# Two attention layers joined: layer 2's last batch and layer 3's first two steps in one sequence of instructions

## The reference, cut to what matters

```
x = layernorm(x + L0(x, adj))   # 8 Euler steps of a linear graph ODE
x = layernorm(x + L1(x, adj))   # graph convolution, two batch norms over all batches and nodes
x = layernorm(x + L2(x, adj))   # 4-head attention masked by adj, head size 32
x = layernorm(x + L3(x, adj))   # one-head graph attention

L3:  Wh = h @ W;  s1 = Wh @ a1;  s2 = Wh @ a2
     e = leaky_relu(s1[:, :, None] + s2[:, None, :], 0.2), masked where adj == 0
     out = softmax(e) @ Wh
```

## Time and profile before

| | |
|---|---|
| median of 3 runs | 1016.34 us (1015.45 to 1021.12) |
| profiled execution | 1015.21 us, its span 1013.3 us |
| PE, DVE, ACT, POOL busy | 90%, 64%, 49%, 38% |
| mean granted TensorE clock | 0.952 of 2.4 GHz |

### The profile page before, as it was taken

One profiled execution on the slowest core, in us unless ns is written; L12 is line 12 of the kernel. 1 busy time (PEld: TensorE's weight loads), 2 busy tenths in 40 slices (PEclk: granted clock), 3 DMA queues, 4 the chain that ended last, 5 costly groups with the idle time before them and its releaser, 6 DMA issues. The chain is left out here.

```text
span 1013.3 us, 20934 instructions
## 1 busy us (share of the span) xinstructions
PE 911.3 (90%) x6036; PEld 643.4 (63%) x6036; DVE 646.4 (64%) x2016; ACT 501.3 (49%) x900; POOL 388.1 (38%) x440
## 2 busy tenths in 40 slices
PE   6999999999999899764799999999999937999994
PEld 5799999999998788332454455444544415667663
DVE  4745554555455866464567777777777415988984
ACT  4321212212112355553477777777776624767762
POOL 4001021111111210002367777778777640455445
PEclk9999999999999999895699999999999977999997
DMA  8000000000000000000342423333333300010111
GB/s 234 21 11 12 22 12 18 13 10 21 10 0 18 22 0 1 0 0 1 68 90 65 94 63 84 72 80 77 78 79 78 80 3 1 22 31 21 31 31 31
DMA packets 34217, 40.63 MB, mean 40 GB/s; under 512 B 6656, under 2 KB 17536, under 8 KB 34176
## 3 DMA queue, kind: packets, MB, share of 16 engines
q1 hardware_dynamic: 33072, 40.00, 16.5%
q10 hardware_dynamic: 1104, 0.13, 0.1%
HBM read 6.43 MB, written 4.19 MB: 10 GB/s over the span
## 5 line engine op out<-in xcount | busy, mean ns | idle before, releaser
L1319 DVE CUSTOM_DVE_ANT_0 junk<-bank,mask_ij 128x512 bf16<-128x512 f32 x256 | 166.7, 689 | 82.7 <-PE bank L1396 81.1
L1199 POOL TENSOR_TENSOR half_sum<-prob 128x1024 f32<-128x1024 f32 x64 | 151.8, 2381 | 11.6 <-ACT prob L1262 11.6
L1262 ACT ACTIVATE prob<-wide 128x1024 f32<-128x1024 f32 x128 | 125.2, 1017 | 37.8 <-PE wide L1413 32.5
L424 ACT CAST yT<-wide 128x512 fp32r<-128x512 f32 x48 | 28.1, 588 | 206.2 <-PE wide L809 156.8
L1396 PE MATMUL bank<-qkT 32*128 32x512 f32 x256 | 66.9, 518 | 20.5 <-DVE mx L1319 17.8
L519 POOL TENSOR_TENSOR Xr<-Xf,Xr 128x512 fp32r<-128x512 f32 x16 | 20.4, 1291 | 168.1 <-ACT Xr L419 167.9
L152 POOL TENSOR_SCALAR n_rstd<-n_aggr 128x4 f32<-128x4 f32 x32 | 6.7, 209 | 198.6 <-DVE n_aggr L145 186.6
L1409 PE MATMUL wide<-qk_st 128*128 128x512 f32 x256 | 76.7, 422 | 0.7 <-ACT prob L1262 0.3
L1732 PEld LDWEIGHTS bank<-Wh,pr 128*128 128x128 f32 x512 | 61.1, 196 | 23.8 <-issue 19.9
L1732 PE MATMUL bank<-Wh,pr 128*128 128x129 f32 x512 | 65.3, 282 | 10.9 <-ACT pr L1600 10.9
L58 PE MATMUL bank<-z,L3T_hi 128*128 128x256 f32 x256 | 73.3, 286 | 1.0 <-DVE z L625 0.9
(11 more groups left out here) (282 smaller groups left out, 2278.9 us busy)
## 6 DMA issues: line engine op xcount, KB each, us to landing
qk_st<-qkT SPq DMA_DIRECT2D x192, 128.0 KB, 2.4
out_dram<-rc SPq DMA_DIRECT2D x16, 256.0 KB, 2.3
Xf<-X SPq DMA_DIRECT2D x14, 256.0 KB, 2.3
A<-in_adj_dram SPq DMA_DIRECT2D x4, 256.0 KB, 5.2
qk_st<-neg_row SPq DMA_DIRECT2D x64, 2.0 KB
Xf<-in_x_dram SPq DMA_DIRECT2D x2, 256.0 KB, 6.7
mask_q<-mask_ji SPq DMA_DIRECT2D x16, 32.0 KB, 1.8
w<-in_L_gnn_W_dram SPq DMA_DIRECT2D x2, 128.0 KB, 2.2
```

The lines of the kernel that those rows point to most:

```text
L1199: pool.tensor_tensor(flat(half_sum[h][:]), flat(prob[bp][h][:, 0:2]), flat(prob[bp][h][:, 2:4]), ALU.add).then_inc(h_sum, 1)
L1262: act.activation(flat(prob[bp][h][:, 2 * half:2 * half + 2]), wide[half][:], ACT.Exp, scale=SCALE).then_inc(t_exp, 1)
L1319: dve.tensor_tensor_reduce(out=junk[hh][:], in0=bank[4 + hh][:], in1=m.mask_ij[:, i], scale=1.0, scalar=3.0 * MASKED, op0=ALU.add, op1=ALU ...
```

## The change

Layers 2 and 3 share one block (`layers2_3`). Each engine runs layer 2's steps up to 17 or 18 as before, then a list written out by hand (`tail`), in which words with a leading 3 are items of layer 3 (`3x0.1` is item x0 of batch 1) and the others items of layer 2, and then layer 3's loop from step 2. Layer 3's large buffers lie at fixed places over layer 2's input `m.O`, over `qk_st` and over `qkT`. Layer 3's weights are loaded and prepared in layer 0's last step: two more transfers on SP behind that of `m.W2`, a wait and a transpose at the end of TensorE's `#w`, a copy on VectorE, a small matmul and copy (`#v`), and two copies on ScalarE that spread the columns. The items of layer 3 are otherwise unchanged, and its waits for layer 2 are three: all Exps of batch 15 ahead of its first transpose, the norm of the batch that GpSimd copies, and the last use of `m.O`.

```diff
--- before.py
+++ after.py
-def pairs(eng, steps, depth, step):
+def pairs(eng, steps, depth, step, first=0, last=None):
...
-    for s in range(lead):
+    for s in range(first, lead):
...
-    for s in range(steps, steps + depth - 1):
+    for s in range(steps, steps + depth - 1 if last is None else last + 1):
...
-            "PE": order("#t0 #t1 #t2 #t3 #w0 p p p p #A0 #A1 #A2 #A3 p p p p"),
+            "PE": order("#t0 #t1 #t2 #t3 #w0 p p p p #A0 #A1 #A2 #A3 p p p p #v0"),
             "ACT": order("z z z z #t0 #t1 #t2 #t3 #x0 #x1 z z z z #A0 #A1 #A2 #A3"),
-            "DVE": order("z z N z z A #m0 #m1 p p #m2 #m3 #G0 p p #D0 z z z z #A0 #x0 #x1 #w0 p #A1 p #A2 p #A3 p n #a0 a"),
+            "DVE": order("z z N z z A #m0 #m1 p p #m2 #m3 #G0 p p #D0 z z z z #A0 #x0 #x1 #w0 p #A1 p #A2 p #A3 p n #v0 #a0 a"),
         }
...
-        LATE = {"PE": ORDER, "ACT": ORDER, "DVE": order("N #x2 #a1 A")}
+        LATE = {"PE": ORDER, "ACT": order("#v0"), "DVE": order("N #x2 #a1 A")}
...
+            sp.dma_start(m.WX[:, 0:D], ins["L3_gnn_W"]).then_inc(w3_in, 16)
+            with nc.allow_non_contiguous_dma(reason="256 words once"):
+                sp.dma_start(L1.a3[:], ins["L3_gnn_a"].rearrange("(k p) a -> p (k a)", p=P)).then_inc(w3_in, 16)
...
+            sp.wait_ge(w3_in, 2 * 16)
...
+                    elif what == "#v":
+                        act.wait_ge(wa_c, 1)
+                        for n in range(2):
+                            act.activation(m.wB[n][:], m.WX[:, D + n:D + n + 1].broadcast_to([P, P]), ACT.Copy).then_inc(wb_c, 1)
...
+                        dve.wait_ge(wt_ps, 1)
+                        dve.tensor_copy(L1.W3T[:], bank[3][:, 0:D]).then_inc(wt_c, 1)
+                    elif what == "#v":
+                        dve.wait_ge(wa_ps, 1)
+                        dve.tensor_copy(m.WX[:, D:D + 2], bank[3][:, 0:2]).then_inc(wa_c, 1)
...
+                        pe.wait_ge(w3_in, 2 * 16)
+                        pe.transpose(bank[3][:, 0:D], m.WX[:, 0:D], m.ident[:]).then_inc(wt_ps, 1)
+                    elif what == "#v":
+                        pe.wait_ge(wt_c, 1)
+                        pe.matmul(bank[3][:, 0:2], L1.W3T[:], L1.a3[:], start=True, stop=True).then_inc(wa_ps, 1)
...
+        m.WX = at("WX", [P, D + 2])
+        m.wB = [at(f"wB{k}", [P, P]) for k in range(2)]
...
+def layer3(nc, own, m, bank, out, rl1_at, ready):
...
+    at = [172352]
...
+    WX, wB = m.WX, m.wB
+    Xf = [over(f"Xc{k}", [P, NT, D]) for k in range(2)]
+    xT = [over(f"xTc{k}", [P, N]) for k in range(2)]
+    Wh = [over(f"Wh{k}", [P, NT, D + 2]) for k in range(2)]
+    junk = [over(f"junk3{k}", [P, N], BF16) for k in range(2)]
+    dg = [over(f"dg{k}", [P, NT, P], BF16) for k in range(2)]
+    r = [over(f"rc{k}", [P, NT, D]) for k in range(2)]
+    onesb = over("onesb", [P, P], BF16)
+    rl = [over("rl0", [P, NT, N]), nc.alloc_sbuf_tensor_at("rl1", [P, NT, N], F32, offset=rl1_at)]
+    at[0] = 205120
+    pr = [over(f"pr{k}", [P, NT, N]) for k in range(2)]
+    s12 = [sb(f"s12{k}", [P, NT, 2]) for k in range(2)]
+    s2s = [sb(f"s2s{k}", [P, 2, NT]) for k in range(2)]
...
+    def pool_constants(pool):
+        pool.sem_inc(x_f, CREDIT)
+        norm.credit_pool(pool)
+        norm.credit_apply(pool)
+        pool.wait_ge(*ready["O"])
+        for n, ap in enumerate((onesb[:], Wh[0][:, :, D:D + 1], Wh[1][:, :, D:D + 1])):
+            pool.memset(ap, 1.0).then_inc(const, 1)
+
+    def pool_copy(pool, s, par, first=False):
+        pool.wait_ge(x_ps, after(s - 2, 1))
+        pool.wait_ge(ready["X"], after(s, 4))
+        if not first:
+            pool.wait_ge(norm.s_x, after(s - 4, 4))
+        hold(pool, gate)
+        pool.tensor_copy(flat(Xf[par][:]), batch_flat(m.X, s)).then_inc(x_f, 1)
+
+    def pool_norm(pool, b, par, copied):
+        pool.wait_ge(x_f, after(copied, 1))
+        norm.root(pool, b + CREDIT, par)
+        norm.apply(pool, b + CREDIT, par, r[par], lambda k: r[par][:, k])
+
+    def pool_rest(pool):
...
+                if isinstance(s, int) and s == 0:
+                    pe.wait_ge(*ready["score banks"])
...
+        third = layer3(nc, own, m, bank, out, qkT_at,
+                       {"O": (bn, after(B - 1, 1)), "X": norm.s_x, "score banks": (t_exp, after(B - 1, EXPS))})
...
+        def tail(text, items, second, third_item):
+
+            backs = dict(items)
+            for word in text.split():
+                name, b = word.split(".")
+                b = int(b)
+                if name[0] == "3":
+                    s = b + third.STAGE[name[1]]
+                    third_item(name[1], int(name[2]), s, s % 2, s // 2)
+                else:
+                    s = b + backs[name]
+                    second(name, b, b % 2, s, [0 <= s - k < B for k in range(6)])
 
...
-            run(pool, POOL_ORDER, work)
+            run(pool, POOL_ORDER, work, last=17)
+            third.pool_constants(pool)
+            for b in range(2):
+                third.pool_copy(pool, b, b, first=True)
+            tail("r.14 S2.15 S3.15 g2.14", POOL_ORDER, work, None)
+            third.pool_copy(pool, 2, 0, first=True)
+            tail("r.15 g2.15", POOL_ORDER, work, None)
+            third.pool_copy(pool, 3, 1, first=True)
+            third.pool_norm(pool, 0, 0, 3)
+            third.pool_rest(pool)
...
-            run(act, ACT_ORDER, work)
+            run(act, ACT_ORDER, work, last=18)
+            third.act_credits(act)
+            item = third.act_items(act)
+            tail("3x0.0 f.15 3w0.0 3w1.0 y.14 3l0.0 3l1.0 e.15 3l2.0 3l3.0 3g0.0 3x0.1 3w0.1 3w1.1 3E0.0 3E1.0 "
+                 "3l0.1 3l1.1 3l2.1 3l3.1 3g0.1 y.15", ACT_ORDER, work, item)
+            pairs(act, B, 3, third.in_order(item), first=2)
...
-            run(dve, DVE_ORDER, work)
+            run(dve, DVE_ORDER, work, last=17)
+            third.dve_credits(dve)
+            item = third.dve_items(dve)
+            tail("b.14 3w0.0 3w1.0 3m0.0 3m1.0 3m2.0 3m3.0 3c0.0 3c1.0 3c2.0 c1.15 c2.15 3e0.0 3e1.0 3w0.1 3w1.1 b.15 "
+                 "3e2.0 3e3.0 3m0.1 3m1.1 3m2.1 3m3.1 3c0.1 3c1.1 3c2.1", DVE_ORDER, work, item)
+            pairs(dve, B, 3, third.in_order(item), first=2)
...
-            run(pe, PE_ORDER, work)
...
+            run(pe, PE_ORDER, work, last=18)
+            third.pe_credits(pe)
+            item = third.pe_items(pe)
+            pe.wait_ge(third.const, 3)
+            tail("3x0.0 V0.15 V1.15 V2.15 V3.15 3w0.0 3w1.0 3j0.0 3i0.0 o.15 D0.15 D1.15 3x0.1 d.15 3w0.1 3w1.1 3e0.0 3e1.0 "
+                 "3j0.1 3i0.1 3e2.0 3e3.0", PE_ORDER, work, item)
+            pe.wait_ge(rcp, after(B - 1, 1))
+            pe.wait_ge(o_n, after(B - 1, 1))
+            pairs(pe, B, 3, third.in_order(item), first=2)
...
```

More of the change, by code:

```diff
@@ L277, in layer0 @@
         blocks_in = sem("mask_blocks_in"); const = sem("rows_set")
+        w3_in = sem("w3_in"); wt_ps = sem("WT_in_psum"); wt_c = sem("WT_out"); wa_ps = sem("Wa_in_psum"); wa_c = sem("Wa_out")
+        wb_c = sem("Wa_spread")
         Hb, Xa, agT, W1T = L1.Hb, L1.Xr, L1.agT, L1.W1T
@@ L908, in aggregate_step @@
                         pe.wait_ge(la_w_lo, 1)
+                        pe.wait_ge(wa_c, 1)
                         pe.wait_ge(h_sb, after(groups - 1, 2 * NT))
@@ L957, in __init__ @@
         self.wf = at("wf", [P, CH, P])
+        self.a3 = at("a_sb", [P, 2])
+        self.W3T = at("WT", [P, D])
         self.at = 170304
@@ L1066, in layer2, with layers2_3 @@
+def layers2_3(nc, m, bank, wide, out):
     SCALE = float(HD) ** -0.5
@@ L1079, in layer2 @@
         xTr = [sb(f"xT_{h}", [P, N], F32R) for h in ("hi", "lo")]
+        qkT_at = nc.sbuf_base
         qkT = [sb(f"qkT{k}", [P, 4, N], F32R) for k in range(2)]
@@ L1135, in released, with run @@
                     "o": (o_n, after(b, 1)), "T": (res1, after(b, 1))}[name]
-        def run(eng, items, act_on):
+        def run(eng, items, act_on, last=None):
             depth = 1 + max(back for _, back in items)
@@ L1144, in step @@
                         act_on(name, s - back, (par + back) % 2, s, alive)
-            pairs(eng, B, depth, step)
+            pairs(eng, B, depth, step, last=last)
+        def tail(text, items, second, third_item):
[6 more added lines that the diff above has]
+                    third_item(name[1], int(name[2]), s, s % 2, s // 2)
+                else:
+                    s = b + backs[name]
+                    second(name, b, b % 2, s, [0 <= s - k < B for k in range(6)])
         @block.sync
@@ L1172, in _ @@
             run(sp, SP_ORDER, transfer)
+            third.sync(sp)
         @block.gpsimd
@@ L1755, in build @@
             layer1_rest(nc, second, m, bank, L1)
-            layer2(nc, m, ins, bank, wide)
-        layer3(nc, m, ins, bank, out)
+            layers2_3(nc, m, bank, wide, out)
 _INS = ["x", "adj", "L0_gnn_alpha_train", "L0_gnn_w", "L0_gnn_d", "L0_gnn_fc_in_w", "L0_gnn_fc_in_b",
```

479 lines of the change are left out of this document (216 added, 263 removed).

## The result

| | before | after |
|---|---|---|
| median of 4 runs each, us | 1015.89 (1013.87 to 1021.12) | 1000.87 (995.78 to 1005.56) |
| profiled execution, its span, us | 1015.21, 1013.3 | 995.78, 994.0 |
| mean granted clock of TensorE in it | 0.952 | 0.967 |

The medians differ by 15.0 us. The ratio of the times, after over before, is 0.9839 with a 95% interval of 0.9803 to 0.9876, so the gain is clear of no change and between 1.2% and 2.0%. The forecast was 1002, range 995.5 to 1009.

A forecast was written before the change was run, and what follows sets the result against it. The layer 2 to 3 stretch was held bound by latency, not an engine; -21.3 + 0.3 + 3.0 + 3.3 + 0.5 = -14.2 us from 1015.2 gave 1001.0, stated as 1002 against the runs' median, range 995.5 to 1009.

The forecast's parts named there:

- join without the clock: Layer 2's last Exp to layer 3's first `a`: 20.7 us in place of 42.0, so 21.3 less.
- y.15 in step 2: Layer 3's step 2: ScalarE runs y.15 (1.65 us) ahead of batch 2's input copy; 0.3 us is left as cost.
- clock in three gaps: TensorE's clock may fall behind three idle times in the join; +3.0 us taken, bounds 0 and 4.6.
- wait for `a` in layer 0: Layer 0: TensorE waits for the last-issued transfer, so products `p` start 3.3 us late; bounds 0 and 5.6.
- other pieces in layer 0: Layer 0: an added VectorE copy and small matmul, with ScalarE's copies within the bounds; +0.5 us, bounds 0 and 1.
- orders that are passed: Join: items moved ahead of others, such as GpSimd's memsets and copies, cost 0, bounds 0 and +1 us.
- the transfer is hidden: Rival in layer 0: the weights' transfer costs nothing, the 3.3 us fall away, 998.8 us; chance 0.14.
- gap 3: TensorE idle ahead of layer 3's first `a`, 3.4 us; a clock fall there would cost 1.5 to 1.9 us.
- gap 1: TensorE idle ahead of batch 0's transposes, 2.1 us; a clock fall would cost about half of 1.4 us.
- gap 2: TensorE idle ahead of batch 1's projections, 2.4 us; a clock fall would cost about half of 1.4 us.
- cold loop: Rival: layer 3's loop from step 2 stays at low clock, +6.7 us per step, 1022 after three; chance 0.04.
- interlocked orders: Rival in the join: in-order queues wait on each other in turn, wholly or in half, 1007 to 1015; chance 0.11.

The follow-up runs named there:

- in_turn: Changed kernel, still one block, but each engine runs all of layer 2's list before layer 3's; 1013.61 us, ratio 0.9964 to the kernel before.
- two_gaps: Changed kernel with layer 3's weight transfers issued earlier and unread matmuls (9, 8) in TensorE's first two join gaps only; 994.90 us, ratio 0.9778 to before.
- all_together: Changed kernel with earlier weight transfers, three join gaps filled, y.15 and b.15 moved later, sums' masks ahead of score rows; 997.17 us, ratio 0.9781 to before.
- fill_gaps: Changed kernel plus 9, 8 and 11 unread matmuls in TensorE's three idle gaps of the join; 995.73 us, ratio 0.9808 to the kernel before.
- early_and_fill: Changed kernel with layer 3's weight transfers issued right behind layer 1's and all three join gaps filled with unread matmuls; 994.24 us, ratio 0.976 to before.
- late_and_fill: Changed kernel with layer 3's W transposed, and its transfers awaited, behind A's four transposes, and three join gaps filled; 996.57 us, ratio 0.9775 to before.

## Why the prediction was right, step by step

| step | predicted | measured |
|---|---|---|
| join without the clock | -21.3 (20.7 for 42.0) | -21.55 (20.45); 20.64 to 20.69 with gaps filled |
| y.15 in step 2 | +0.3 | +0.2 |
| step 3 | 0 | +0.4, cause open |
| clock in three gaps | +3.0 (0 to 4.6) | 0, 4.2, 2.9, 2.9, 2.9, 0 in six traces: mean 2.2 |
| wait for `a` in layer 0 | +3.3 | +3.27 |
| other pieces in layer 0 | +0.5 | +0.4 at A's transposition, +0.7 at the statistics |
| orders that are passed | 0 (0 to +1) | no wait in the join shows a cost |
| sum | -14.2 | -14.8 with +4.0 for layer 0; -15.0 by the medians |

- *The join was right for the reason given.* The distances from the last Exp, predicted and measured: TensorE through with the denominators 9.1 and 9.55; ScalarE through with batch 1's input 12.8 and 13.0; VectorE's first sum 14.5 and 14.8, its last ended 19.4 and 19.2; first `a` 20.7 and 20.45. Running the written orders against each other by hand, at the durations of rows, placed each of these to half a microsecond. in_turn shows that the order, not the shared block, brings most of it.
- *The layer 0 wait was right in mechanism and size,* 2.48 us from issue to use where 2.27 was taken. That the start of `p` came out to 0.02 us (325.95 foretold, 325.93 found) is luck: TensorE got `a` 0.3 later than foretold, at 325.80, and `p` began 0.13 behind the start of the transposition, not 0.45. The rival that the transfer is hidden fell.
- *The orders passed cost nothing, but with less cover than I said.* I had GpSimd's half sums end 3.0 us behind the last Exp; they ended 4.83 behind it, since GpSimd stood idle 2.15 us ahead of its first copies of X. The prediction let only copies 2 and 3 wait for `x_ps`; but the starting credit of `x_ps` is given by TensorE, behind its last items of step 18 (L1326, the releaser in the row at 814.30). This is also a wait of layer 3 for layer 2 beyond the three that the section on the change counts. The half sums' reader, the denominators, came 7.63 behind the last Exp, so 2.8 us of cover remained of the four.
- *The clock term came out near its size (2.2 for 3.0) with its parts wrong, so in part by luck.* I held gap 3, the longest in my schedule at 3.4 us, the likeliest and dearest, and took half of 1.4 for each of the other two. Gap 3 was 2.3 to 2.8, and the clock fell behind it in one of seven traces in which it was not filled (two_gaps). The clock fell at gaps 1 and 2 in four of six traces each. At gap 1, with the whole of the values' 3.6 us behind it, a fall cost 2.9 once and 1.7 three times; at gap 2 it cost 1.2 each time. I sized a fall at a gap by the gap's length; how much work runs at the low clock behind it counts as much.
- *The profiled execution flatters the change.* It is the fastest of the four and lost no clock in the join. Its trace alone says -19.3; the medians say -15.0. The difference of 4.3 is about what the join's clock costs on average (2.2) and the 2.3 by which the unchanged stretches came out shorter in that trace. To read the size of a change from one pair of traces would have missed by more than a quarter.
- The rivals of a cold loop and of interlocked orders did not come: the steps are 9.71, 9.95 and 9.52. (VectorE's list, given as 25 items there, has 26; nothing hangs on it.)

## What to carry to other kernels

Where two stages meet and no engine is full, interleaving their in-order lists can be worth more than removing the boundary. Here it took 13.2 us off the join where the clock held and 10.5 by the medians, against 8.4 for the boundary and the set-up together, of which layer 0 took 4 back. Its worth could be worked out beforehand from rows, with every engine's list run against the others. A small transfer added for later use goes to the head of its queue or its wait behind work that is ready: here the one in last place held TensorE 3.7 us. Where short idle gaps of TensorE remain, price what runs behind them at the low clock; unread matmuls in gaps 1 and 2 went with a clock that held there in five traces of five, against two of six without them (about 1.8 us of the join, 4 by the ratios, whose intervals overlap). But they must be sized anew with each change of the order, or they delay what they protect (1.7 us in all_together).

## What the runs showed of the hardware

- The same gap in the same program may or may not cost the clock. Gap 1, 2.31 us long in both traces of the kernel after, kept 2.4 GHz in one and fell to 1.2 GHz in the other; over six traces with near the same order it fell in this gap or within 1.5 us behind it in four. The Trainium skill ("TensorE: Matmul & The Clock Gate", HAM oscillation — how this bites in real kernels) advises, for matmuls with few rows that wait for their data, to restructure the loop so that TensorE stays warm. The rows here agree in that much: with the three gaps filled the clock is 1.00 through the join in fill_gaps, early_and_fill, late_and_fill and all_together.
- The time of one program moves in levels. From layer 1's first statistics to layer 2's last Exp, where the orders are the same but for a few items near the end, eight traces took 398.6 to 399.9 us and six 401.8 to 404.2; from the third `a` to the end, three levels: 134.4, 136.0 and 137.3 (each within 0.1). With the join filled the runs form two groups in early_and_fill, 991.4 to 992.2 us at a mean granted clock of 0.968 to 0.970 and 996.3 to 997.6 at 0.960 to 0.963. What decides which way a run goes was not found.
